# Routing shares brought to the rows of an expert tile by repeating DMA reads in place of a selection matmul

## The chip, the core and the metric

The kernel runs on one core of a Trainium2 chip, alone. The metric is the device time of one execution in microseconds (us). The engines named here are TensorE (PE, with PEld for its weight loads), VectorE (DVE), ScalarE (ACT), GpSimd (POOL) and SyncE (SP), whose queue issues the DMAs.

## What is computed

The program is a decoder of two layers over 32 sequences of 128 tokens with 128 features: attention, cross attention over a context and a feed forward part, twice, each added to x after a layer norm. The part that matters here is the last one, a mixture of experts on 4096 tokens:

```python
scores = sigmoid(x @ gate_w.T) + gate_bias                 # 64 experts
# the 4 best of 8 groups of experts, then the 6 best experts in them, their scores made to sum to 1
comb   = zeros((T, 64)).at[arange(T)[:, None], topk_i].add(topk_w)   # the routing shares
h      = silu(einsum('th,eih->eti', x, eg_w)) * einsum('th,eih->eti', x, eu_w)   # 64 hidden rows an expert
routed = einsum('eti,ehi,te->th', h, ed_w, comb)
shared = silu(x @ sg_w.T) * (x @ su_w.T) @ sd_w.T          # one expert of 128 rows for all tokens
x      = x + shared + routed
```

Every expert is computed for every token, and its hidden values are multiplied by the token's share for it, which is zero for 58 of 64 experts.

## The kernel before

Each engine has its own hand written order of work, and semaphores tie the orders together. The stages follow one another: attention, the wide cross attention, feed forward, attention, cross attention, experts. While the last cross attention runs, SP also loads the expert weights (`load_experts`, line 2096) and GpSimd splits each into a high part `w_hi`, rounded to fp32r, and the remainder `w_lo` (`split_experts`, line 639). A product in full precision is then three matmuls, high by high, high by low and low by high (`three`, line 1440).

The experts' stage takes the tokens in 8 groups (`G`) of 4 sequences, 512 tokens. Two experts of 64 rows make one tile of 128 partitions, so a group has 32 expert tiles and, as tile 32, the shared expert (`NT` = 33). For tile k the work is:

- TensorE, `project` (line 1445): three gate matmuls into one PSUM bank, three up matmuls into another, and for k < 32 one selection matmul (line 1461). Its weights `pick` are a 0/1 matrix that copies the high and the low part of the share of expert 2k to the upper 64 partitions and of expert 2k+1 to the lower 64, and sums them, into a third bank. Then `project_down` of tile k - 3 (`LAG` = 3): three matmuls.
- ACT: silu of the gate bank (line 1540), and `high_part` of tile k - 2, the copy of h to fp32r (`h_hi`, line 1547).
- VectorE: `product` of tile k, up bank times silu, into `h1` (line 1675); then `hidden` of tile k - 1 (line 1678), the share times `h1`, into `h` (line 1685); for tile 32 a plain copy (line 1688).
- GpSimd: `low_part`, h minus h_hi, into `h_lo` (line 1737), which the down matmuls need beside `h_hi`.

Everything in that list has two buffers by tile (`h_hi` and `h_lo` three): gate and up of tile k wait for silu and product of tile k - 2, the selection matmul for hidden of tile k - 2, hidden of tile k for h_lo of tile k - 2.

Beside this, group g prepares group g + 1: VectorE normalises it behind tile 2, TensorE transposes it behind tile 7 and computes the scores behind tile 9 (ACT changes its table to sigmoid and back there), GpSimd splits the inputs behind tile 10 (line 1731), VectorE does one of 16 routing steps behind each of the tiles 11 to 26 (`route`, line 1601). Behind tile 27 it splits the shares into a high and a low half (`split_shares`, lines 1665 and 1667), behind tile 29 TensorE transposes them (line 1436) and ACT copies them to `share_t` (line 1534). At the start of the stage all of that stands in line before tile 0 of group 0. SP only stores each finished group to the output (line 2117).

Of the kernel before, what the change touches and what calls it, by code (L numbers as in the profile page):

```python
# [638 lines left out]
def split_experts(pool, nc, m, s, k, u):  # L639

    at = slice(k * 128, k * 128 + 128) if isinstance(k, int) else bass.ds(k * 128, 128)
    pool.wait_ge(s.raw[u], 16 + 8 * (k - u))
    nc.gpsimd.tensor_copy(m.w_hi[:, :, at], m.raw[:, u, 0:3, :]).then_inc(s.split_hi, 1)
    if not (isinstance(k, int) and k == B):
        nc.gpsimd.tensor_copy(m.pick[:, at], m.raw[:, u, 3, :])
    pool.wait_ge(s.split_hi, k + 1)
    nc.gpsimd.tensor_tensor(m.w_lo[:, :, at], m.raw[:, u, 0:3, :], m.w_hi[:, :, at].bitcast(F32),
                            ALU.subtract).then_inc(s.split, 1)
# [388 lines left out]
GB = 4  # L1037
# [349 lines left out]
NT = E // 2 + 1  # L1387
LAG = 3
class ExpertSemaphores:

    def __init__(self, sem, stage):
        self.normed = sem(f"{stage}_normed")
        self.x_t = sem(f"{stage}_x_t")
        self.x_f = sem(f"{stage}_x_f")
        self.x_hi = sem(f"{stage}_x_hi")
        self.x_lo = sem(f"{stage}_x_lo")
        self.logits = sem(f"{stage}_logits")
        self.scores = sem(f"{stage}_scores")
        self.routed = sem(f"{stage}_routed")
        self.shares_t = sem(f"{stage}_shares_t")  # L1400
        self.shares = sem(f"{stage}_shares")
        self.gated = sem(f"{stage}_gated")
        self.upped = sem(f"{stage}_upped")
        self.shared_out = sem(f"{stage}_shared_out")
        self.silus = sem(f"{stage}_silus")
        self.products = sem(f"{stage}_products")
        self.hiddens = sem(f"{stage}_hiddens")
        self.his = sem(f"{stage}_his")
        self.los = sem(f"{stage}_los")
        self.downed = sem(f"{stage}_downed")  # L1410
        self.out_s = sem(f"{stage}_out_s")
        self.out_t = sem(f"{stage}_out_t")
        self.updated = sem(f"{stage}_updated")
# [4 lines left out]
def moe_tensor(pe, nc, m, s):  # L1418
# [14 lines left out]
    def transpose_shares(g):  # L1433
        pe.wait_ge(s.routed, g + 1)
        for q in range(GB):
            last = nc.tensor.transpose(m.misc[:, q * 128:q * 128 + 128], m.share[:, q, :].bitcast(F32),
                                       m.ident[:])
        last.then_inc(s.shares_t, 1)
# [6 lines left out]
    def project(g, u, k):  # L1445
        n, tile = NT * g + k, slice(128 * k, 128 * k + 128)
        if k == 0:
            pe.wait_ge(s.x_hi, g + 1)
            pe.wait_ge(s.x_lo, g + 1)
        wait(pe, s.silus, n - 1)  # L1450
        x_hi, x_lo = m.x_hi[:, u, :], m.x_lo[:, u, :]
        three(m.gate_bank[(k + u) % 2][:], m.w_hi[:, 0, tile], m.w_lo[:, 0, tile], x_hi, x_lo)\
            .then_inc(s.gated, 1)
        wait(pe, s.products, n - 1)
        three(m.up_bank[(k + u) % 2][:], m.w_hi[:, 1, tile], m.w_lo[:, 1, tile], x_hi, x_lo)\
            .then_inc(s.upped, 1)
        if k < NT - 1:
            wait(pe, s.hiddens, n - 1)
            if k == 0:
                pe.wait_ge(s.shares, g + 1)  # L1460
            nc.tensor.matmul(m.share_bank[(k + u) % 2][:], m.pick[:, tile], m.share_t[:, u, :],  # L1461
                             start=True, stop=True).then_inc(s.shared_out, 1)

# [15 lines left out]
    def body(g, u):  # L1479
        before, after = group_exists(g - 1), group_exists(g + 1)  # L1480
        for k in range(NT):
            project(g, u, k)
            if k >= LAG:
                project_down(g, k - LAG)
            elif before:
                project_down(g - 1, k - LAG + NT)
            if k == 5 and before:
                transpose_output(g - 1)
            if k == 7 and after:
                wait(pe, s.updated, GB * g)  # L1490
                transpose_inputs(g + 1)
            if k == 9 and after:
                logits(g + 1)
            if k == 29 and after:
                transpose_shares(g + 1)
# [25 lines left out]
def moe_scalar(act, nc, m, s):  # L1521
# [9 lines left out]

    def copy_shares(g, u):
        act.wait_ge(s.shares_t, g + 1)
        nc.scalar.copy(m.share_t[:, u, :], m.misc[:]).then_inc(s.shares, 1)

# [17 lines left out]
    def body(g, u):  # L1553
        before, after = group_exists(g - 1), group_exists(g + 1)
        for k in range(NT):
# [9 lines left out]
            if k == 9 and after:  # L1565
                routing_scores(g + 1)
            if k == 29 and after:
                copy_shares(g + 1, 1 - u)

    copy_inputs(0)  # L1570
    routing_scores(0)
    copy_shares(0, 0)
    over_groups(act, body)
# [8 lines left out]
def moe_vector(dve, nc, m, s):  # L1582
# [18 lines left out]
    def route(g, n):  # L1601
# [5 lines left out]
        if n == 0:  # L1607
            dve.wait_ge(s.scores, g + 1)
            last = nc.vector.tensor_tensor(rows(m.sc, E), rows(m.sg, E),
                                           m.gate_b[:].unsqueeze(1).broadcast_to([128, GB, E]), ALU.add)  # L1610
# [50 lines left out]

    def split_shares(g):
        dve.wait_ge(m.s.route, ROUTE_STEPS * (g + 1))
        wait(dve, s.shares_t, g)
        nc.vector.tensor_copy(m.share[:, :, 0:E], rows(m.w, E)).then_inc(m.s.halves, 1)
        dve.wait_ge(m.s.halves, g + 1)
        nc.vector.tensor_tensor(m.share[:, :, E:2 * E], rows(m.w, E), m.share[:, :, 0:E].bitcast(F32),
                                ALU.subtract).then_inc(s.routed, 1)

    def product(g, u, k):  # L1670
# [7 lines left out]
    def hidden(g, u, k):  # L1678
# [4 lines left out]
        if k < NT - 1:  # L1683
            dve.wait_ge(s.shared_out, (NT - 1) * g + k + 1)
            nc.vector.tensor_tensor(m.h[:, here, :], m.share_bank[here][:], m.h1[:, here, :], ALU.mult)\  # L1685
                .then_inc(s.hiddens, 1)
        else:
            nc.vector.tensor_copy(m.h[:, here, :], m.h1[:, here, :]).then_inc(s.hiddens, 1)
# [8 lines left out]
    def body(g, u):  # L1697
        before, after = group_exists(g - 1), group_exists(g + 1)
        for k in range(NT):
# [11 lines left out]
            if 11 <= k < 11 + ROUTE_STEPS and after:  # L1711
                route(g + 1, k - 11)
            if k == 27 and after:
                split_shares(g + 1)

    normalise(0)
    split_inputs(0, 0)
    for n in range(ROUTE_STEPS):
        route(0, n)
    split_shares(0)  # L1720
    over_groups(dve, body)
# [4 lines left out]
def moe_pool(pool, nc, m, s):  # L1726
# [24 lines left out]
    low_part(G - 1, 1, NT - 1)  # L1751

# [52 lines left out]
def program(nc, io, out):  # L1807
    arena = ExitStack()
    with arena:
# [88 lines left out]
        with ExitStack() as part:  # L1898
            over = placer(part)
            m.pick = over("pick", [128, (NT - 1) * 128], F32R)  # L1900
        m.score_w = sb("score_w", [128, XH, C])
        m.out_w = sb("out_w", [128, XH, C])

        with ExitStack() as part:
            over = placer(part)
            m.raw = over("raw", [128, 2, 4, 128])
        m.wug = sb("wug", [128, 2 * FT * C])
# [34 lines left out]
        with ExitStack() as part:  # L1942
# [4 lines left out]
            m.x_lo = over("x_lo", [128, 2, 512], F32R)  # L1947
            m.share_t = over("share_t", [128, 2, 512], F32R)
            m.share = over("share", [128, GB, 2 * E], F32R)
            m.sl = over("sl", [128, 2, 512])  # L1950
# [46 lines left out]
        m.mixed, m.back, m.asked = bank[4], bank[5], bank[7]  # L1997
        m.gate_bank, m.up_bank, m.share_bank, m.out_bank, m.misc = bank[0:2], bank[2:4], bank[4:6], bank[6], bank[7]

# [14 lines left out]
        m.s.route = sem("all_route")  # L2014
        m.s.halves = sem("all_halves")
        m.s.stored = sem("all_stored")
# [27 lines left out]
        for n, (a, a.k_diag, a.q_pack, a.v_store) in enumerate(stages):  # L2044
            a.q_rows, a.k_rows = (nc.dram_tensor(f"{side}_rows{n}", (2, HC, ROWS, NC, 2 * T), F32, kind="Internal").ap()
                                  for side in "qk")
            a.ones = nc.dram_tensor(f"ones{n}", (128 - MAXIMA, SLOTS * H * a.columns), F32, kind="Internal").ap()
            a.ones_in = 16 * (n + 1)

        def row(name, p=128):  # L2050
# [25 lines left out]
        with nc.Block() as block:  # L2076
            @block.sync
            def _(sp):
# [35 lines left out]
                load_experts(B, 0)  # L2114
                with sp.Fori(0, G) as g:
                    sp.wait_ge(s5.updated, GB * g + GB)
                    sp.dma_start(out[bass.ds(g * GB, GB)].rearrange("b t c -> t b c"),
                                 x_view[:, bass.ds(g * GB, GB), :]).then_inc(m.s.stored, 16)
                sp.wait_ge(m.s.stored, 16 * G)
# [136 lines left out]
def layouts(w):  # L2256
# [14 lines left out]
    def up(a, shared):  # L2271
        return np.concatenate([a.reshape(E // 2, 128, C), shared[None]]).transpose(0, 2, 1)

    down = np.concatenate([w["L1_ffn_ed_w"].reshape(E // 2, 2, C, 64).transpose(0, 1, 3, 2).reshape(E // 2, 128, C),
                           w["L1_ffn_sd_w"].T[None]])
    expert = 2 * np.arange(NT)[:, None] + np.arange(128)[None, :] // 64
    pick = (np.arange(128)[None, :, None] % E == expert[:, None, :]).astype(np.float32)
    experts = np.stack([up(w["L1_ffn_eg_w"], w["L1_ffn_sg_w"]), up(w["L1_ffn_eu_w"], w["L1_ffn_su_w"]),
                        down, pick], 2)
    out = {"bias_columns": np.concatenate([columns("L0_attn_b_attn", (0, 1)), columns("L1_xattn_bq", (0,)),  # L2280
# [29 lines left out]
```

## Time and profile before

| | |
|---|---|
| median of 3 runs | 2505.26 us (2498.2 to 2507.59) |
| profiled execution | 2503.74 us, span 2501.9 us |
| mean granted clock of TensorE | 0.923 |
| busy share of the span | PE 88%, PEld 73%, DVE 65%, ACT 56%, POOL 38% |
| selection matmul, line 1461 | 256 matmuls of 512 columns |
| experts' stage | from about 1853 us to the end |

The page gives busy time by engine, then the span in 40 slices, the DMA queues, the chain of work that ended last, and the costliest groups of instructions with what ended the idle time before them. "bank" is a PSUM bank. Matmuls are pipelined: the times at which they start tell more than their durations. An operation's duration includes the time in which it stands on its engine and can't read its operands.

### The profile page before, as it was taken

To read this page: it belongs to the slowest core of one execution; us is meant where nothing else is said; L and a number is where in the kernel's file an instruction comes from. 1 tells how busy PE (TensorE), PEld (TensorE's weight loads), DVE (VectorE), ACT (ScalarE), POOL (GpSimd) and SP (SyncE) were. 2 spreads that over 40 slices of the span, in tenths; PEclk is the share of its full clock that TensorE was granted. 3 is DMA by queue.
4 is the path that set the end of the run, shared out by engine and by line. 5 is a ranking of instruction groups with operands and counts; after the bars stand their busy time and mean duration, and the time that the engine had idled before them with its cause. 6 is when DMAs were issued, how large, how long until landed. Compare 5 with 4: busy or idle time off the path is not lost.

```text
span 2501.9 us, 52319 instructions
## 1 busy us (share of the span) xinstructions
PE 2194.1 (88%) x16155; PEld 1824.7 (73%) x16241; DVE 1634.5 (65%) x3705; ACT 1395.2 (56%) x3390; POOL 949.5 (38%) x1125
## 2 busy tenths in 40 slices
PE   1999989999999999970269999688879999999998
PEld 0677679999999999830147776466547888888887
DVE  2566657666776666679855665466547677776775
ACT  0455457777777777755415554355535555555554
POOL 2111124444444444305321110233315555555555
PEclk9999979999999999985569999588859999999999
DMA  8333300000000000000023332355510000000000
GB/s 201 121 121 120 100 1 2 0 0 0 0 0 0 0 0 0 1 0 0 0 77 104 116 120 71 105 152 153 149 32 1 5 5 6 2 4 5 5 5 5
DMA packets 178614, 111.78 MB, mean 45 GB/s; under 512 B 31619, under 2 KB 173891, under 8 KB 178371
## 3 DMA queue, kind: packets, MB, share of 16 engines
q1 hardware_dynamic: 178491, 110.30, 15.2%
q8 instruction: 57, 0.93, 0.2%
q14 instruction: 66, 0.54, 0.1%
HBM read 68.82 MB, written 42.10 MB: 44 GB/s over the span
## 4 chain that ended last, share of the span: by engine, by line
PE 79%; SPq 8%; DVE 6%; issue 3%; DMA 2%; ACT 1%; POOL 1%; DVEq 0%; POOLq 0%; ACTq 0%
PE bank L1441 7%; PE bank L1443 7%; PE bank L1442 7%; PE bank L239 6%; PE bank L719 5%; PE bank L720 5%; PE bank L721 5%; PE bank L713 5%; PE bank L764 4%; PE bank L742 4%; PE bank L250 4%; PE bank L221 3%; SPq L599 3%; PE bank L1461 2%; PE bank L237 2%
## 5 line engine op out<-in xcount | busy, mean ns | idle before, releaser
L1737 POOL TENSOR_TENSOR h_lo<-h,h_hi 128x512 fp32r<-128x512 f32 x264 | 340.5, 1290 | 284.8 <-ACT h_hi L1547 284.8
L427 DVE TENSOR_REDUCE nm<-bank 128x4 f32<-128x512 f32 (+1 forms) x384 | 238.0, 621 | 294.4 <-PE bank L221 293.2
L361 ACT ACTIVATE pt<-bank 128x512 f32<-128x512 f32 (+1 forms) x384 | 228.8, 596 | 285.9 <-PE bank L239 281.0
L982 POOL TENSOR_TENSOR pw<-ew,rw 128x410 f32<-128x410 f32 x256 | 223.2, 872 | 372.3 <-DVE rw L904 372.3
L1540 ACT ACTIVATE sl<-bank 128x512 f32<-128x512 f32 x264 | 157.9, 598 | 275.1 <-PE bank L1443 273.0
L1675 DVE TENSOR_TENSOR h<-bank,sl 128x512 f32<-128x512 f32 x264 | 182.0, 689 | 174.8 <-PE bank L1443 148.1
L239 PE MATMUL bank<-q_pack,k_diag 128*128 128x128 f32 (+1 forms) x1536 | 269.4, 302 | 24.3 <-DMA q_pack<-nmt 24.3
L239 PEld LDWEIGHTS bank<-q_pack,k_diag 128*128 128x128 f32 (+1 forms) x1536 | 215.6, 191 | 63.9 <-DMA q_pack<-nmt 25.8
L908 DVE TENSOR_TENSOR pwt_lo<-bank,pwt_hi 128x512 fp32r<-128x512 f32 x256 | 176.9, 691 | 78.9 <-ACT pwt_hi L836 78.8
L221 PE MATMUL bank<-k_diag,q_pack 128*128 128x512 f32 (+1 forms) x384 | 210.3, 552 | 13.9 <-DMA k_diag<-k_rows 12.0
L827 ACT ACTIVATE ew<-bank,nmax 128x205 f32<-128x205 f32 x512 | 217.7, 434 | 1.0 <-DVE nmax L896 0.9
L1441 PE MATMUL bank<-x_hi,w_hi 128*128 128x512 f32 x528 | 209.3, 396 | 0.0
L1443 PE MATMUL bank<-x_hi,w_lo 128*128 128x512 f32 x528 | 206.5, 391 | 0.0
L1442 PE MATMUL bank<-x_lo,w_hi 128*128 128x512 f32 x528 | 206.2, 391 | 0.0
L250 PE MATMUL bank<-pt,vx 128*32 128x128 f32 (+1 forms) x3072 | 172.7, 299 | 2.6 <-ACT pt L361 1.9
L1685 DVE TENSOR_TENSOR h<-bank,h 128x512 f32<-128x512 f32 x256 | 174.0, 680 | 0.2 <-DVE h L1675 0.2
L842 ACT COPY us<-bank 128x256 f32<-128x256 f32 x256 | 95.3, 372 | 124.7 <-PE bank L721 123.5
L1547 ACT CAST h_hi<-h 128x512 fp32r<-128x512 f32 x264 | 161.7, 612 | 3.2 <-DVE h L1685 1.6
L713 PE MATMUL bank<-kvt,score_w 128*128 128x128 f32 x1024 | 158.1, 277 | 1.7 <-DVE qs_lo L913 0.9
L719 PE MATMUL bank<-kvt_hi,qs_hi 128*128 128x206 f32 x512 | 158.8, 310 | 0.0
L546 POOL COPY vx<-v_store 128x128 f32 (+3 forms) x96 | 27.8, 290 | 344.5 <-PE bank L250 344.5
L742 PE MATMUL bank<-ident,pw 128*128 128x128 f32 x1024 | 154.2, 273 | 3.2 <-POOL pw L982 2.1
(278 smaller groups left out, 5962.3 us busy)
## 6 DMA issues: line engine op xcount, KB each, us to landing
q_pack<-q_rows SPq DMA_DIRECT2D x96, 256.0 KB, 3.1
k_diag<-k_rows SPq DMA_DIRECT2D x256, 64.0 KB, 2.6
q_rows<-q_hi SPq DMA_DIRECT2D x96, 128.0 KB, 2.1
k_rows<-k_hi SPq DMA_DIRECT2D x96, 128.0 KB, 2.1
raw<-in_experts SPq DMA_DIRECT2D x33, 256.0 KB, 2.7
q_rows<-q_lo SPq DMA_DIRECT2D x48, 128.0 KB, 2.1
k_rows<-k_lo SPq DMA_DIRECT2D x48, 128.0 KB, 2.1
k_diag<-k_rows SPq DMA_DIRECT2D x128, 39.0 KB, 2.5
```

The lines of the kernel that those rows point to most:

```text
L221: nc.tensor.matmul(bank, a.q_pack[:, u, c, :], a.k_diag[:, u, c, :, 0:a.columns], start=a.mask is None, stop=True)\
L239: last = nc.tensor.matmul(bank[0:a.keys, 128 * h:128 * h + 128], a.k_diag[:, u, c, h, 0:a.keys], a.q_pack[:, u, c, :], start=a.mask is Non ...
L250: last = nc.tensor.matmul(m.mixed[ROWS * h:ROWS * h + ROWS, 128 * c:128 * c + 128], m.vx[0:a.keys, u % 2, HC * c + h, :], m.pt[0:a.keys, c ...
L361: nc.scalar.activation(m.pt[0:a.keys, c % 2, :, :].rearrange("p h t -> p (h t)"), m.flip[c % 2][0:a.keys, :], ACT.Exp).then_inc(s.exped.se ...
L427: nc.vector.tensor_reduce(m.nm[:, u % 2, :].rearrange("p (h c) -> p c h", c=NC)[:, c, :], m.score[c % 2][:, 0:HC * a.columns].rearrange("p ...
L713: last = nc.tensor.matmul(m.ask[:, 128 * k:128 * k + 128], m.score_w[:, 2 * c + k, :], m.kvt[:, u, 0:T], start=True, stop=True)
L719: nc.tensor.matmul(out, left_hi, right_hi, start=first, stop=False)
L742: last = nc.tensor.transpose(m.flip[0][:, at:at + 128], m.pw[:, c % 2, k, 128 * part:128 * part + 128], m.ident[:])
L1441: nc.tensor.matmul(bank, w_hi, x_hi, start=first, stop=False)
L1442: nc.tensor.matmul(bank, w_hi, x_lo, start=False, stop=False)
L1443: return nc.tensor.matmul(bank, w_lo, x_hi, start=False, stop=last)
L1737: nc.gpsimd.tensor_tensor(m.h_lo[:, k % 3, :], m.h[:, (k + u) % 2, :], m.h_hi[:, k % 3, :].bitcast(F32), ALU.subtract).then_inc(s.los, 1)
```

## The change

The share no longer goes through TensorE. VectorE doesn't split the shares, and TensorE transposes the routing weights of two sequences at a time (2 transposes of 128 columns in place of 4), behind tile 28 in place of 29. ACT copies them to `share_t`, now 128x256 fp32. SP writes `share_t` to a DRAM scratch `share_rows` of 64 experts by 512 tokens with two DMAs, waits for both, and then, for each of the 32 tiles, issues one DMA that reads the two rows of the tile's experts 64 times over and writes 128 partitions of 512 fp32 values (256 KB) to one of four buffers, `share_b`. The load for tile k waits until hidden of tile k - 4 is done. VectorE's hidden of tile k waits for that load and multiplies `share_b` by `h1`; both of its inputs now lie in SBUF. The stores to the output move into the same row of SP's work, behind the load of tile 12 of the next group.

Because the repeated read gives expert 2k to the even partitions and expert 2k + 1 to the odd ones, the rows of the two experts of a tile are interleaved in the weights, on the host. The matrix `pick` is gone from the inputs: an expert's load has 192 KB in place of 256, and GpSimd's copy of it (line 645) goes.

```diff
-    nc.gpsimd.tensor_copy(m.w_hi[:, :, at], m.raw[:, u, 0:3, :]).then_inc(s.split_hi, 1)
-    if not (isinstance(k, int) and k == B):
-        nc.gpsimd.tensor_copy(m.pick[:, at], m.raw[:, u, 3, :])
+    nc.gpsimd.tensor_copy(m.w_hi[:, :, at], m.raw[:, u, :, :]).then_inc(s.split_hi, 1)
...
     def transpose_shares(g):
-        pe.wait_ge(s.routed, g + 1)
-        for q in range(GB):
-            last = nc.tensor.transpose(m.misc[:, q * 128:q * 128 + 128], m.share[:, q, :].bitcast(F32),
-                                       m.ident[:])
+        pe.wait_ge(m.s.route, ROUTE_STEPS * (g + 1))
+        for q in range(GB // 2):
+            last = nc.tensor.transpose(m.misc[:, q * 128:q * 128 + 128], m.w[:, q * 128:q * 128 + 128], m.ident[:])
         last.then_inc(s.shares_t, 1)
...
-        if k < NT - 1:
-            wait(pe, s.hiddens, n - 1)
-            if k == 0:
-                pe.wait_ge(s.shares, g + 1)
-            nc.tensor.matmul(m.share_bank[(k + u) % 2][:], m.pick[:, tile], m.share_t[:, u, :],
-                             start=True, stop=True).then_inc(s.shared_out, 1)
...
-            if k == 29 and after:
+            if k == 28 and after:
...
-    def copy_shares(g, u):
+    def copy_shares(g):
         act.wait_ge(s.shares_t, g + 1)
-        nc.scalar.copy(m.share_t[:, u, :], m.misc[:]).then_inc(s.shares, 1)
+        wait(act, s.rows_saved, 32 * g)
+        nc.scalar.copy(m.share_t[:], m.misc[:, 0:256]).then_inc(s.shares, 1)
...
-    def split_shares(g):
-        dve.wait_ge(m.s.route, ROUTE_STEPS * (g + 1))
-        wait(dve, s.shares_t, g)
-        nc.vector.tensor_copy(m.share[:, :, 0:E], rows(m.w, E)).then_inc(m.s.halves, 1)
-        dve.wait_ge(m.s.halves, g + 1)
-        nc.vector.tensor_tensor(m.share[:, :, E:2 * E], rows(m.w, E), m.share[:, :, 0:E].bitcast(F32),
-                                ALU.subtract).then_inc(s.routed, 1)
...
         if k < NT - 1:
-            dve.wait_ge(s.shared_out, (NT - 1) * g + k + 1)
-            nc.vector.tensor_tensor(m.h[:, here, :], m.share_bank[here][:], m.h1[:, here, :], ALU.mult)\
+            dve.wait_ge(s.share_in[k % SHARES], 16 * ((NT - 1) // SHARES * g + k // SHARES + 1))
+            nc.vector.tensor_tensor(m.h[:, here, :], m.share_b[:, k % SHARES, :], m.h1[:, here, :], ALU.mult)\
                 .then_inc(s.hiddens, 1)
...
+def moe_sync(sp, m, s, out, x_view):
+
+    def save_shares(g, u):
+        sp.wait_ge(s.shares, g + 1)
+        for k in range(2):
+            sp.dma_start(m.share_rows[u].rearrange("e (p k t) -> k e p t", k=2, t=T)[k],
+                         m.share_t[E * k:E * k + E, :]).then_inc(s.rows_saved, 16)
+
+    def load_share(g, u, k):
+        if k == 0:
+            sp.wait_ge(s.rows_saved, 32 * g + 32)
+        wait(sp, s.hiddens, NT * g + k - SHARES + (k >= SHARES))
+        pair = m.share_rows[u, 2 * k:2 * k + 2, :].rearrange("e t -> (e t)").unsqueeze(0).broadcast_to([64, 2 * 512])
+        sp.dma_start(m.share_b[:, k % SHARES, :], pair).then_inc(s.share_in[k % SHARES], 16)
+
+    def store(g):
+        sp.wait_ge(s.updated, GB * g + GB)
+        first = g * GB if isinstance(g, int) else None
+        dst = out[first:first + GB] if isinstance(g, int) else out[bass.ds(g * GB, GB)]
+        src = x_view[:, first:first + GB, :] if isinstance(g, int) else x_view[:, bass.ds(g * GB, GB), :]
+        sp.dma_start(dst.rearrange("b t c -> t b c"), src).then_inc(m.s.stored, 16)
+
+    def body(g, u):
+        save_shares(g, u)
+        for k in range(NT - 1):
+            load_share(g, u, k)
+            if k == 12 and group_exists(g - 1):
+                store(g - 1)
+
+    over_groups(sp, body)
+    store(G - 1)
...
-            m.pick = over("pick", [128, (NT - 1) * 128], F32R)
+            m.share_b = over("share_b", [128, SHARES, 512])
...
-            m.share_t = over("share_t", [128, 2, 512], F32R)
-            m.share = over("share", [128, GB, 2 * E], F32R)
+            m.share_t = over("share_t", [128, 256])
...
+        m.share_rows = nc.dram_tensor("share_rows", (2, E, 512), F32, kind="Internal").ap()
...
-        return np.concatenate([a.reshape(E // 2, 128, C), shared[None]]).transpose(0, 2, 1)
-
-    down = np.concatenate([w["L1_ffn_ed_w"].reshape(E // 2, 2, C, 64).transpose(0, 1, 3, 2).reshape(E // 2, 128, C),
+        pairs = a.reshape(E // 2, 2, 64, C).transpose(0, 2, 1, 3).reshape(E // 2, 128, C)
+        return np.concatenate([pairs, shared[None]]).transpose(0, 2, 1)
+
+    down = np.concatenate([w["L1_ffn_ed_w"].reshape(E // 2, 2, C, 64).transpose(0, 3, 1, 2).reshape(E // 2, 128, C),
                            w["L1_ffn_sd_w"].T[None]])
-    expert = 2 * np.arange(NT)[:, None] + np.arange(128)[None, :] // 64
-    pick = (np.arange(128)[None, :, None] % E == expert[:, None, :]).astype(np.float32)
     experts = np.stack([up(w["L1_ffn_eg_w"], w["L1_ffn_sg_w"]), up(w["L1_ffn_eu_w"], w["L1_ffn_su_w"]),
-                        down, pick], 2)
+                        down], 2)
```

## Rows read from the trace of the kernel before

**Rows 1.** Busy time by stretch: engines with counts, granted clock, DMA share, GB/s.

```profile
1872.30:2491.00 618.70, 617.21 (x2757) 504.87 (x2757) 446.69 (x826) 324.81 (x569) 346.40 (x268) 1.00 0.01 4
```

**Rows 2.** Order in time, TensorE, two group ends: start, us, engine, line, operation.

```profile
2040.55 0.60 PE L1475 MATMUL bank<-ident,yt 128*128 128x128 f32 x4
2040.90 0.48 PE L1441 MATMUL bank<-x_hi,w_hi 128*128 128x512 f32 x1
...
2118.38 0.60 PE L1475 MATMUL bank<-ident,yt 128*128 128x128 f32 x4
```

**Rows 3.** Order in time, all engines, one plain tile of group 2.

```profile
2100.15 0.39 PE L1441 MATMUL bank<-x_hi,w_hi 128*128 128x512 f32 x1
...
2101.03 0.60 ACT L1540 ACTIVATE sl<-bank 128x512 f32<-128x512 f32 x1 [1.17 <-PE bank L1443]
...
2101.52 0.61 ACT L1547 CAST h_hi<-h 128x512 fp32r<-128x512 f32 x1
2101.72 0.69 DVE L1675 TENSOR_TENSOR h<-bank,sl 128x512 f32<-128x512 f32 x1 [0.98 <-PE bank L1443]
...
2102.21 1.29 POOL L1737 TENSOR_TENSOR h_lo<-h,h_hi 128x512 fp32r<-128x512 f32 x1 [0.98 <-ACT h_hi L1547]
2102.32 0.68 DVE L1685 TENSOR_TENSOR h<-bank,h 128x512 f32<-128x512 f32 x1
...
2103.98 0.69 DVE L1675 TENSOR_TENSOR h<-bank,sl 128x512 f32<-128x512 f32 x1 [0.98 <-PE bank L1443]
```

**Rows 4.** The instructions of line 1643: ns least/median/most, first and last start.

```profile
L1643 DVE TENSOR_TENSOR sa<-ms,m x8: 426/862/862, 1864.3 to 2391.7; 128x256 f32<-128x256 f32 x8
```

**Rows 5.** Order in time, VectorE and GpSimd, a routing step of group 2.

```profile
2074.55 1.29 POOL L1737 TENSOR_TENSOR h_lo<-h,h_hi 128x512 fp32r<-128x512 f32 x1 [0.97 <-ACT h_hi L1547]
...
2075.26 0.86 DVE L1634 TENSOR_TENSOR ms<-sc,gq 128x256 f32<-128x256 f32 x1
```

**Rows 6.** Order in time, the last tile's plain copy.

```profile
2493.01 0.43 DVE L1688 COPY h<-h 128x512 f32<-128x512 f32 x1 [0.58 <-POOL h_lo L1737]
...
2493.16 2.65 POOL L1737 TENSOR_TENSOR h_lo<-h,h_hi 128x512 fp32r<-128x512 f32 x2 [0.26 <-ACT h_hi L1547]
...
2494.62 0.19 PEld L1441 LDWEIGHTS bank<-h_hi,w_hi 128*128 128x128 f32 x1 [1.13 <-POOL h_lo L1737]
```

**Rows 7.** Order in time, VectorE and GpSimd at a splitting of inputs.

```profile
2056.00 1.29 POOL L1737 TENSOR_TENSOR h_lo<-h,h_hi 128x512 fp32r<-128x512 f32 x1 [0.23 <-ACT h_hi L1547]
...
2056.61 0.97 DVE L1609 TENSOR_TENSOR sc<-sg,gate_b 128x256 f32<-128x256 f32 x1
...
2057.26 1.47 POOL L1731 TENSOR_TENSOR x_lo<-xf,x_hi 128x512 fp32r<-128x512 f32 x1
```

**Rows 8.** The tile raw: its instructions, ns least/median/most, and who waits.

```profile
L2099 SPq DMA_DIRECT2D raw<-in_experts x33: 328/430/765, 1607.1 to 1837.5; - x33
...
L645 POOL CAST pick<-raw x32: 288/291/295, 1610.5 to 1837.9; 128x128 f32 x20, 128x128 fp32r<-128x128 f32 x12
...
  DMA raw<-in_experts: 136.9, 29
```

**Rows 9.** DMA issues: count, KB each, median us to landing.

```profile
q_pack<-q_rows SPq DMA_DIRECT2D x96, 256.0 KB, 3.1
...
q_rows<-q_hi SPq DMA_DIRECT2D x96, 128.0 KB, 2.1
...
bases<-in_L_xattn_bproj SPq DMA_DIRECT2D x1, 64.0 KB, 3.0
```

**Rows 10.** Order in time, start of the experts' stage.

```profile
1868.86 0.43 DVE L1667 TENSOR_TENSOR share<-w,share 128x256 fp32r<-128x256 f32 x1
...
1869.35 1.12 PE L1436 MATMUL bank<-ident,share 128*128 128x128 f32 x4 [10.11 <-DVE share L1667]
...
1876.25 0.68 DVE L1685 TENSOR_TENSOR h<-bank,h 128x512 f32<-128x512 f32 x1
```

**Rows 11.** Busy time by stretch, in the cross attention.

```profile
1740.00:1760.00 20.00, 17.15 (x178) 12.30 (x181) 13.29 (x33) 11.23 (x25) 8.37 (x16) 0.89 0.49 142
```

More of the change, by code:

```diff
@@ L642, in split_experts @@
     pool.wait_ge(s.raw[u], 16 + 8 * (k - u))
-    nc.gpsimd.tensor_copy(m.w_hi[:, :, at], m.raw[:, u, 0:3, :]).then_inc(s.split_hi, 1)
-    if not (isinstance(k, int) and k == B):
-        nc.gpsimd.tensor_copy(m.pick[:, at], m.raw[:, u, 3, :])
+    nc.gpsimd.tensor_copy(m.w_hi[:, :, at], m.raw[:, u, :, :]).then_inc(s.split_hi, 1)
     pool.wait_ge(s.split_hi, k + 1)
-    nc.gpsimd.tensor_tensor(m.w_lo[:, :, at], m.raw[:, u, 0:3, :], m.w_hi[:, :, at].bitcast(F32),
+    nc.gpsimd.tensor_tensor(m.w_lo[:, :, at], m.raw[:, u, :, :], m.w_hi[:, :, at].bitcast(F32),
                             ALU.subtract).then_inc(s.split, 1)
@@ L1388 @@
 LAG = 3
+SHARES = 4
 class ExpertSemaphores:
@@ L1398, in __init__ @@
         self.scores = sem(f"{stage}_scores")
-        self.routed = sem(f"{stage}_routed")
         self.shares_t = sem(f"{stage}_shares_t")
@@ L1403, in __init__ @@
         self.upped = sem(f"{stage}_upped")
-        self.shared_out = sem(f"{stage}_shared_out")
+        self.rows_saved = sem(f"{stage}_rows_saved")
+        self.share_in = [sem(f"{stage}_share_in{k}") for k in range(SHARES)]
         self.silus = sem(f"{stage}_silus")
@@ L1566, in body @@
                 routing_scores(g + 1)
-            if k == 29 and after:
-                copy_shares(g + 1, 1 - u)
+            if k == 28 and after:
+                copy_shares(g + 1)
     copy_inputs(0)
     routing_scores(0)
-    copy_shares(0, 0)
+    copy_shares(0)
     over_groups(act, body)
@@ L1608, in route @@
             dve.wait_ge(s.scores, g + 1)
+            wait(dve, s.shares_t, g)
             last = nc.vector.tensor_tensor(rows(m.sc, E), rows(m.sg, E),
@@ L1712, in body @@
                 route(g + 1, k - 11)
-            if k == 27 and after:
-                split_shares(g + 1)
     normalise(0)
@@ L1719, in moe_vector @@
         route(0, n)
-    split_shares(0)
     over_groups(dve, body)
@@ L1905, in program @@
             over = placer(part)
-            m.raw = over("raw", [128, 2, 4, 128])
+            m.raw = over("raw", [128, 2, 3, 128])
         m.wug = sb("wug", [128, 2 * FT * C])
@@ L1997, in program @@
         m.mixed, m.back, m.asked = bank[4], bank[5], bank[7]
-        m.gate_bank, m.up_bank, m.share_bank, m.out_bank, m.misc = bank[0:2], bank[2:4], bank[4:6], bank[6], bank[7]
+        m.gate_bank, m.up_bank, m.out_bank, m.misc = bank[0:2], bank[2:4], bank[6], bank[7]
         m.s, m.es = Names(), Names()
@@ L2014, in program @@
         m.s.route = sem("all_route")
-        m.s.halves = sem("all_halves")
         m.s.stored = sem("all_stored")
@@ L2114, in _ @@
                 load_experts(B, 0)
[L2115 to L2118, printed above, removed]
+                moe_sync(sp, m, s5, out, x_view)
                 sp.wait_ge(m.s.stored, 16 * G)
```

## The prediction

> **What bounds the kernel now.** I read the 40 slices first, then the stage table, the groups by shape, and the order in time of single tiles. The change lies in the last stage, the experts (8 groups of 33 tiles), and in the copies made for it one stage earlier. From 1872 to 2491 us TensorE is busy 617.2 of 618.7 us at a granted clock of 1.00 (its 2.4 GHz level); VectorE is busy 72% and GpSimd 56% [rows 1]. A tile is a gapless row of ten 512-wide matmuls: three gate, three up, one selection, three down. VectorE's products of two tiles start 2.26 us apart (2101.72 to 2103.98), so a matmul is worth 0.226 us [rows 3]. The output transposes of two groups start at 2040.55 and 2118.38, so a group takes 77.8 us [rows 2].
>
> The reader must also see how little room there is beside TensorE. In [rows 3] the gate matmuls start at 2100.15, silu at 2101.03, the h_hi copy at 2101.52, the product at 2101.72, GpSimd's h_lo subtraction (1.29 us) at 2102.21, the multiplication by the share ("hidden") at 2102.32. The last two lie over each other, and hidden's 0.68 us doesn't suffer. Its inputs there are one PSUM bank and h1.
>
> **Part 1, the selection matmul goes.** 32 tiles x 8 groups = 256 matmuls x 0.2265 us = 58.0 us of TensorE, all on the path [rows 3]. Two of four share transposes a group go too: four took 0.35 us of the row (2040.55 to 2040.90) [rows 2], so 0.17 us x 8 = 1.4 us. With nothing else late, a tile takes 9 x 0.2265 = 2.04 us.
>
> **Part 2, hidden reads two SBUF tensors.** This decides the case. Before, the share came from PSUM; now share_b and h1 are both in SBUF, while h_lo (two SBUF inputs on GpSimd) runs beside it. The trace has this pair in another place, the routing. A 128x256 VectorE operation with two SBUF inputs takes 426 ns at least and 862 in the median of eight [rows 4]. The short ones lie at the start of the stage, where no h_lo runs yet (0.43 us at 1868.86 [rows 10]); in a running group the same kind starts at 2075.26 and ends at 2076.12, 0.28 us after the h_lo beside it (2074.55 + 1.29 = 2075.84) [rows 5]. Against 0.43 us for 256 elements, 0.69 us for 512 [rows 3] is 0.26 more, so I take hidden at 0.69 us when free and at 0.55 us after the end of h_lo when blocked.
>
> It works the other way round too. The copy of 2493.01 ends at 2493.44; the subtraction issued at 2493.16 frees its matmul only at 2494.62, so ends about 1.13 us after the copy [rows 6]. In [rows 7] the VectorE addition, issued at 2056.61 during an h_lo, ends at 2057.58, and the next GpSimd subtraction, issued at 2057.26, ends at 2058.73, 1.15 us later. Here VectorE got its turn between two GpSimd operations: who asks first goes first. So: blocked h_lo ends 1.15 us after VectorE's operation.
>
> The Trainium skill (SBUF — State Buffer, "Who interferes with whom") says the same of a VectorE operation with both inputs in SBUF against GpSimd's reads, and says the pair of ports is held for the whole instruction. The trace agrees on the blocking but not on the last point: taken literally, the blocked 256-wide operation would end 0.43 us after h_lo, and the row shows 0.28. By the page's version both blocked terms below would be 0.14 us longer, the cycle 7.41 us instead of 7.13, and the run some 24 us slower again.
>
> **The cycle that follows.** Waits in the code: down(k) needs h_lo(k), down(k) stands in TensorE's row behind up(k+3) and in front of gate(k+4), VectorE runs product(k+1), hidden(k), ACT runs silu(k+2), h_hi(k). Asked first, goes first: at a 2.04 us pace h_lo(k-2) asks 0.11 us before hidden(k-1), hidden is blocked, its h_hi and h_lo come late, and TensorE waits. Followed tile by tile it settles in a pattern of three tiles. From a late down(k), in us: three down matmuls 0.68; gate start to silu 0.89; silu to h_hi(k+2) 0.49; to h_lo(k+2) 0.69; h_lo 1.29; hidden(k+3), blocked by it, 0.55; handoff to the next product 0.05; to hidden(k+4) 0.60; which asks just before h_lo(k+3) and runs 0.69; blocked h_lo(k+3) 1.15; handoff to down(k+3) 0.05. Sum 7.13 us for three tiles: 2.38 a tile, against 2.26 before and 2.04 of matmuls, with TensorE waiting 1.0 us of every 7.1. Every term is from rows 3 to 7.
>
> I carried the same rules and durations tile by tile through whole groups, with routing steps, the plain copy of tile 32 and the two table loads of ACT in each group. For the kernel before they give 78.5 us a group (measured 77.8 [rows 2]), for the changed one 83.7: +5.2 us. The plain cycle alone gives 33 x 0.12 = 4 us of that; the rest is routing operations in the same queue for the port. Group 0 comes to +4.9, the last group (no routing) to +3.7: 4.9 + 6 x 5.2 + 3.7 = 39.8 us.
>
> Bounds: with the hold of either operation 0.1 us shorter the group comes to 81.0 (+2.5), with GpSimd favoured when both ask 88.1 (+9.6): +20 to +77 us in all. The outer bound below is no blocking at all, rival 1. I take the middle, since the rules meet the group of before within 0.7 us.
>
> **Part 3, the shares through DRAM.** SP has only eight stores in this stage. It now issues 32 loads and two saves a group, 272 in all, at the 0.43 us of an expert load's issue [rows 8]: 117 us in 620, on no other engine. A 256 KB load lands 3.1 us after issue, a save as large as 128 KB 2.1 [rows 9]; a 64 KB bias row repeated over the partitions took 3.0 [rows 9], so a repeated read shows no price of its own. Load k is issued when hidden(k-4) has ended and needed 4 x 2.38 - 0.69 = 8.8 us later. Cost 0; bounds 0 and rival 2. Behind a waiting load on SP stand later loads, the save for the next group and the store of out, which nothing waits for until the end. The last store stays behind the last update. At k = 0 of a later group the chain is transposes, copy, save 2.1, load 3.1, some 7 us, from tile 28 to hidden(0) behind product 1 of the next group, six tiles or 12 us: 0.
>
> At the start the split (its second operation 0.43) and half the slow transposes (1.12 for four) leave the path [rows 10]; save and load come on it. Transposes end near 1869.2, the copy near 1869.6, two saves issued and landed 1872.4, load 1875.5; hidden(0) ran at 1876.25 before [rows 10]. I take 0, bounds -1 and +3.
>
> **Part 4, smaller edits.** The split of the shares leaves VectorE (two operations like the 0.43 of [rows 10] a group): it lay beside matmuls, 0; uncovered it would be -7. The pick copy (0.29 us x 32) and 64 of 256 KB of each expert load leave the stage before. GpSimd waited there 136.9 us for the load, TensorE for other things than these copies [rows 8]: 0; bounds -3 and 0. The interleaved rows cost the same weights and matmuls: 0.
>
> **Sum.** 2503.7 (the profiled execution; span 2501.9) + 39.8 = 2543.5. The median of the three runs is 1.5 above that execution: 2545.
>
> **Rivals.**
> 1. *No blocking for hidden* (each keeps its own pace). Then TensorE is the bound: group 72.0 against 78.5 by the same arithmetic, -6.5 x 8 = -52: 2453. For it: no row shows a 512-wide hidden with two SBUF inputs. Against: rows 4 to 7. This is the other side; it turns where blocking adds less than 0.23 us a tile. Chance 0.14.
> 2. *The shares land late.* Decides above 8.8 us from hidden(k-4); at 12 us each tile takes 0.8 more, +205: 2750. Against it, the slowest row is 3.1. Chance 0.03.
> 3. *The clock falls.* TensorE gets gaps of 1.0 us. The stretch 1740 to 1760, busy 17.2 of 20, had a granted clock of 0.89 in the mean of the two levels 2.4 and 1.2 GHz [rows 11]. If it falls in a fifth of the stage, a tile there takes twice 2.04: 51 tiles x 1.7 = +87 on top: 2632. Against: here one gap of 1.0 us comes in every 7.1, and the stage of before held 1.00 through 1.5 us of gaps [rows 1]. Chance 0.05.
> 4. *The blocking is about worth the matmul*: hidden asks in the gap each time and only 0.22 us a tile is lost. Within 0.5% of before: 2505. Chance 0.06.
>
> The forecast has 0.72, and its own range 2515 to 2582 is from the +20 to +77 above, and a little under it. The whole range, 2497 to 2590, leaves out rivals 1 and 2 and half of 3. A change of 0.5% (12 us) is about what can be told from none. Faster 0.15, same 0.07, slower 0.78.
>
> **What will show it.** Right: hidden on VectorE at two durations, 0.69 and about 1.2 to 1.75; h_lo at 1.29 with some at 1.7; matmuls waiting for h_lo; TensorE idle or late by up to 1.0 us behind h_lo, some 10 to 14% of the stage; clock 1.00; groups 83 us apart; SP waits for hidden, never hidden for a load. Wrong: hidden at 0.69 throughout beside h_lo (then rival 1), or VectorE waiting for DMA (rival 2), or a granted clock under 1 (rival 3). The prediction as a whole is wrong if the group takes under 78 us.

## The result and the profile after

The changed kernel takes 2555.1 us (2552.1 to 2556.0) against 2501.7 us of the kernel before, run beside it: a ratio of 1.021 (95% interval 1.018 to 1.024), slower by 53 us. The prediction had 2545, which is 40 above the 2505 us that it started from. The profiled execution has a span of 2549.9 us.

The stage in question by stretch, columns as in [rows 1]:

```profile
1872.30:2538.00 665.70, 593.64 (x2467) 437.96 (x2466) 585.20 (x808) 332.34 (x562) 377.42 (x268) 1.00 0.33 104
```

TensorE's share fell from 99.8% to 89% and its granted clock stayed at 1.00. VectorE rose from 72% to 88% without more work: the time in which an operation stands blocked counts as busy. The output transposes of two groups, as in [rows 2], give the length of a group, 84.75 us against 77.83:

```profile
2047.23 0.60 PE L1469 MATMUL bank<-ident,yt 128*128 128x128 f32 x4
...
2131.98 0.60 PE L1469 MATMUL bank<-ident,yt 128*128 128x128 f32 x4
```

The tile share_b, with what waited for what (ns least/median/most, then idle us and times):

```profile
L1753 SPq DMA_DIRECT2D share_b<-share_rows x256: 512/513/727, 1864.9 to 2529.4; - x128
L1673 DVE TENSOR_TENSOR h<-share_b,h x256: 678/1584/1731, 1868.1 to 2537.4; 128x512 f32<-128x512 f32 x128
...
  DMA share_b<-share_rows: 1.3, 1
...
  ACT h_hi L1542: 77.0, 118
...
DMA to landing us min/median/max: 2.8/3.2/4.0
```

Here is the answer. The multiplication by the share took 0.68 us before [rows 3]; now it takes 0.68 at least, 1.58 in the median and 1.73 at most. The loads are not late: they land 3.2 us after issue, and VectorE waited for one of 256 loads, the first (1.3 us). The long waits of the stage (who waits for whom, us in total, times, longest):

```profile
ACT h_hi L1542 <- DVE h L1673: 75.5, 117, 1.4
...
PEld bank L1441 <- POOL h_lo L1722: 145.6, 191, 3.0
...
PE bank L1441 <- POOL h_lo L1722: 74.5, 126, 2.6
DVE h L1663 <- PE bank L1443: 53.0, 93, 1.1
```

TensorE and its weight loads stand for h_lo, the h_hi copies for the multiplication. Before, in the same view of the stage, these pairs were short:

```profile
PEld bank L1441 <- POOL h_lo L1737: 5.9, 11, 1.6
...
ACT h_hi L1547 <- DVE h L1685: 1.6, 2, 0.9
```

And last a stretch of plain tiles in group 7, in order of time:

```profile
2502.62 0.50 PE L1441 MATMUL bank<-h_hi,w_hi 128*128 128x512 f32 x1 [0.77 <-POOL h_lo L1722]
2502.66 1.71 DVE L1673 TENSOR_TENSOR h<-share_b,h 128x512 f32<-128x512 f32 x1
...
2502.96 0.39 PE L1442 MATMUL bank<-h_lo,w_hi 128*128 128x512 f32 x1
...
2503.43 0.39 PE L1441 MATMUL bank<-x_hi,w_hi 128*128 128x512 f32 x1
...
2504.32 0.60 ACT L1535 ACTIVATE sl<-bank 128x512 f32<-128x512 f32 x1 [2.00 <-PE bank L1443]
...
2504.81 0.61 ACT L1542 CAST h_hi<-h 128x512 fp32r<-128x512 f32 x1
...
2505.50 1.29 POOL L1722 TENSOR_TENSOR h_lo<-h,h_hi 128x512 fp32r<-128x512 f32 x1 [1.69 <-ACT h_hi L1542]
2505.61 1.73 DVE L1673 TENSOR_TENSOR h<-share_b,h 128x512 f32<-128x512 f32 x1
...
2507.47 0.69 DVE L1663 TENSOR_TENSOR h<-bank,sl 128x512 f32<-128x512 f32 x1
...
2508.07 3.07 POOL L1722 TENSOR_TENSOR h_lo<-h,h_hi 128x512 fp32r<-128x512 f32 x2 [1.28 <-ACT h_hi L1542]
2508.08 0.68 DVE L1673 TENSOR_TENSOR h<-share_b,h 128x512 f32<-128x512 f32 x1
...
2509.95 0.50 PE L1441 MATMUL bank<-h_hi,w_hi 128*128 128x512 f32 x1 [0.77 <-POOL h_lo L1722]
```

Every step of the predicted cycle can be read here. The subtraction of 2505.50 is first, so the multiplication of 2505.61 ends at 2507.34, 0.55 us behind the subtraction's end at 2506.79. Then the multiplication of 2508.08 is first: it takes its free 0.68 us, and the row shows two subtractions from 2508.07 in 3.07 us, where two free ones take some 2.55. (The two rows start 0.01 us apart, h_lo's earlier; that the multiplication went first is read from the durations.) The down matmuls start late at 2502.62 and again at 2509.95: 7.33 us for three tiles, where 7.13 were predicted.

### The profile page after: what moved, and what is told of

The parts are those of the page before. It is cut to its first block, busy times and chain, and to the rows that moved or that the text cites. A ratio compares the mean times of both kernels' runs of the same rounds, so it can differ in the third digit from the quotient of the medians.

```text
span 2549.9 us, 52079 instructions
## 1 busy us (share of the span) xinstructions
PE 2166.3 (85%) x15969; PEld 1756.2 (69%) x15969; DVE 1777.4 (70%) x3689; ACT 1406.7 (55%) x3390; POOL 978.0 (38%) x1093
## 4 chain that ended last, share of the span: by engine, by line
PE 56%; POOL 10%; issue 10%; DVE 9%; SPq 9%; DMA 3%; ACT 2%; POOLq 0%; DVEq 0%; ACTq 0%
POOL h_lo L1722 10%; PE bank L239 5%; PE bank L717 5%; PE bank L718 5%; PE bank L719 5%; PE bank L711 5%; PE bank L762 4%; PE bank L740 4%; PE bank L250 4%; SPq L599 3%; DVE h L1673 3%; PE bank L237 3%; PE bank L221 2%; SPq L575 2%; PE bank L220 2%
## 5 line engine op out<-in xcount | busy, mean ns | idle before, releaser
L1722 POOL TENSOR_TENSOR h_lo<-h,h_hi 128x512 fp32r<-128x512 f32 x264 | 374.1, 1424 | 305.7 <-ACT h_hi L1542 305.0
L1673 DVE TENSOR_TENSOR h<-share_b,h 128x512 f32<-128x512 f32 x256 | 345.4, 1349 | 4.8 <-DVE h L1663 1.3
L1441 PE MATMUL bank<-h_hi,w_hi 128*128 128x512 f32 x264 | 124.2, 470 | 74.6 <-POOL h_lo L1722 74.5
```

The source lines that it names most:

```text
L1441: nc.tensor.matmul(bank, w_hi, x_hi, start=first, stop=False)
L1673: nc.vector.tensor_tensor(m.h[:, here, :], m.share_b[:, k % SHARES, :], m.h1[:, here, :], ALU.mult)\
L1722: nc.gpsimd.tensor_tensor(m.h_lo[:, k % 3, :], m.h[:, (k + u) % 2, :], m.h_hi[:, k % 3, :].bitcast(F32), ALU.subtract).then_inc(s.los, 1)
```

## Experiments

The theory throughout: hidden with two SBUF inputs and the h_lo subtraction on GpSimd shut each other out, first come, first served, and TensorE pays behind h_lo. The rivals: the repeated loads are late or their traffic slows an engine; the interleaving or SP's new work costs it; hidden is slow with two SBUF inputs whatever GpSimd does. The kernel before ran beside each set, at 2500.8 us (e1 to e4) and 2499.9 us (e5 to e7). All kernels but e3 start from the changed one. e2 and e6 multiply by whatever lies in share_b, e3 leaves the shares out, and e4 half of the low parts: their results are not those of the program, and only their times count.

**e1, h1 in PSUM.** One of hidden's two inputs moves to the two banks that the selection matmul left free.

```diff
-        nc.vector.tensor_tensor(m.h1[:, (k + u) % 2, :], m.up_bank[(k + u) % 2][:],
+        nc.vector.tensor_tensor(m.h1_bank[(k + u) % 2][:], m.up_bank[(k + u) % 2][:],
                                 m.sl[:, (k + u) % 2, :], ALU.mult).then_inc(s.products, 1)
...
-            nc.vector.tensor_tensor(m.h[:, here, :], m.share_b[:, k % SHARES, :], m.h1[:, here, :], ALU.mult)\
+            nc.vector.tensor_tensor(m.h[:, here, :], m.share_b[:, k % SHARES, :], m.h1_bank[here][:], ALU.mult)\
...
+        m.h1_bank = bank[4:6]
```

> The changed kernel with one edit: VectorE writes h1, the product of up and silu, to a PSUM bank instead of SBUF, so that hidden reads one SBUF tensor (share_b) and one bank. All DMAs, waits and matmuls stay. Theory (hidden with two SBUF inputs and the h_lo subtraction on GpSimd shut each other out): hidden at 0.68 us throughout, h_lo at 1.29, a group 71.8 us instead of 84.8, some 2448 us in all, so below both kernels. Rival (the repeated loads are late, or their 256 KB a tile slow the engines): no change, 2555, groups 85. Rival (the interleaved weights or the waits of SP cost it): 2555.

Measured: 2460.0 us, ratio to the kernel before 0.984 (0.982 to 0.987). That is 95 us off the changed kernel and 41 us under the kernel before. The pair in order of time, from one tile to the next:

```profile
2099.36 1.30 POOL L1722 TENSOR_TENSOR h_lo<-h,h_hi 128x512 fp32r<-128x512 f32 x1 [1.33 <-ACT h_hi L1542]
...
2099.47 0.68 DVE L1673 TENSOR_TENSOR h<-share_b,bank 128x512 f32<-128x512 f32 x1
...
2101.42 1.29 POOL L1722 TENSOR_TENSOR h_lo<-h,h_hi 128x512 fp32r<-128x512 f32 x1 [0.76 <-ACT h_hi L1542]
...
2101.53 0.68 DVE L1673 TENSOR_TENSOR h<-share_b,bank 128x512 f32<-128x512 f32 x1
```

The subtraction and the multiplication lie over each other as in [rows 3], at 1.29 and 0.68 us, 2.06 us a tile. The stage by stretch, and the output transposes, 72.81 us apart:

```profile
1872.30:2440.00 567.70, 559.51 (x2442) 431.84 (x2443) 425.22 (x803) 316.75 (x557) 342.69 (x265) 1.00 0.40 122
```

```profile
2024.03 0.60 PE L1469 MATMUL bank<-ident,yt 128*128 128x128 f32 x4
...
2096.84 0.60 PE L1469 MATMUL bank<-ident,yt 128*128 128x128 f32 x4
```

Same DMAs, same interleaving, same work of SP: those rivals fall. It is 12 us more than the 2448 expected, with a group at 72.8 for 71.8. The wait that is left:

```profile
PEld bank L1441 <- POOL h_lo L1722: 53.0, 185, 1.7
```

The weights of the down matmuls wait 0.29 us in most tiles, as h_lo now comes only just in time at 2.06 us a tile.

**e2, no loads.** The first four share loads of group 0 are made and the other 252 left out.

```diff
-            load_share(g, u, k)
+            if isinstance(g, int) and g == 0 and k < SHARES:
+                load_share(g, u, k)
...
-            dve.wait_ge(s.share_in[k % SHARES], 16 * ((NT - 1) // SHARES * g + k // SHARES + 1))
+            dve.wait_ge(s.share_in[k % SHARES], 16)
```

> The changed kernel with only the first four share loads of group 0; all 252 others are left out and hidden reads what lies in share_b, so the shares are not those of the routing. Both inputs of hidden stay in SBUF. Theory (VectorE and GpSimd shut each other out): no gain, 2555 within 5 us, hidden's durations spread from 0.68 to 1.7 us as before. Rival (late loads or the DMA traffic): 2450.

Measured: 2556.2 us, ratio 1.022 (1.019 to 1.025). Without the traffic nothing is won, and the multiplication is as slow as with it:

```profile
L1673 DVE TENSOR_TENSOR h<-share_b,h x256: 676/1647/1766, 1873.2 to 2542.4; 128x512 f32<-128x512 f32 x128
```

**e3, the pair in the kernel before.** Nothing of the change but one operand: another SBUF tensor stands where the bank of the share stood.

```diff
-            nc.vector.tensor_tensor(m.h[:, here, :], m.share_bank[here][:], m.h1[:, here, :], ALU.mult)\
+            nc.vector.tensor_tensor(m.h[:, here, :], m.x_hi[:, u, :].bitcast(F32), m.h1[:, here, :], ALU.mult)\
```

> The kernel before, selection matmul and its waits kept, but hidden multiplies h1 by x_hi, an SBUF tensor, instead of by the bank of the share (the shares are left out of the result). No DMA is added. Theory: the blocking alone, with ten matmuls a tile: group 77.8 + 8.6 = 86.4 us by the rules of the prediction, 2502 + 69 = 2571 us. Rival (DMA): as before, 2502.

Measured: 2570.6 us, ratio 1.029 (1.027 to 1.032): 70 us for the blocking with no DMA added, where 69 were expected. The multiplication, and the first line of who waited for it:

```profile
L1685 DVE TENSOR_TENSOR h<-x_hi,h x256: 680/1562/1736, 1872.2 to 2555.9; 128x512 f32<-128x512 f32 x128
...
  PEld bank L1461: 81.4, 149
```

That line also shows where e3 differs from the changed kernel. L1461 is the selection matmul, which waits for the multiplication two tiles back; here most of TensorE's waiting stands there (81.4 us) and only 22.9 us of its weight loads' waits are for h_lo, where the changed kernel, which has no selection matmul, waits for h_lo. So e3 shows that the pair by itself makes the kernel slow, and not what each path costs in the changed kernel. Between the two kernels lie some 15 us, of the 58 that the selection matmul was worth.

**e4, half of h_lo.** GpSimd subtracts 256 of the 512 columns in all tiles but the first three.

```diff
-        nc.gpsimd.tensor_tensor(m.h_lo[:, k % 3, :], m.h[:, (k + u) % 2, :],
-                                m.h_hi[:, k % 3, :].bitcast(F32), ALU.subtract).then_inc(s.los, 1)
+        at = slice(0, 512 if isinstance(g, int) and g == 0 and k < 3 else 256)
+        nc.gpsimd.tensor_tensor(m.h_lo[:, k % 3, at], m.h[:, (k + u) % 2, at],
+                                m.h_hi[:, k % 3, at].bitcast(F32), ALU.subtract).then_inc(s.los, 1)
```

> The changed kernel, but GpSimd's h_lo subtraction covers only 256 of 512 columns (in all tiles but the first three), so it holds the ports about half as long; half of the low parts are left out of the result. In the kernel before its 1.29 us ended ahead of the down matmuls, so by itself it was not on the path. Theory: group 71.7 us, 2450 in all, because a blocked hidden then waits at most 0.6 us and TensorE's 2.04 us a tile bound again. Rival (DMA): 2555. Rival (hidden itself is slower with two SBUF inputs, whatever GpSimd does): 2555.

Measured: 2450.2 us, ratio 0.980 (0.977 to 0.982), as expected. Hidden is still blocked, but for less:

```profile
L1673 DVE TENSOR_TENSOR h<-share_b,h x256: 670/1171/1224, 1870.0 to 2439.3; 128x512 f32<-128x512 f32 x128
```

A multiplication of 1.17 us leaves the kernel 51 us under the one before, one of 1.58 us puts it 53 over. So a slow multiplication is not the price in itself; TensorE pays when h_lo comes late. (A subtraction of 256 columns is itself shorter, 0.74 us in the median for 1.29, and e4 doesn't part this from the shorter blocking.) The rival that hidden is slow by its own inputs falls too: its length follows GpSimd's.

**e5, two buffers.** On top of e1, `SHARES = 2` in place of 4.

```diff
-SHARES = 4
+SHARES = 2
```

> h1 in PSUM and two share buffers in place of four: the load of tile k can be issued only when hidden of tile k - 2 has ended. That leaves 2 x 2.2 - 0.7 = 3.7 us for a wait of SP, an issue of 0.5 us and a landing of 3.2 us after issue. Theory (the loads are hidden by four buffers, with some 4 us to spare): here the spare is used up, 0 to 0.25 us a tile more than with four, 2460 to 2520 us, and VectorE shows waits for the DMA of share_b. Rival (the loads cost something by their traffic, not by their distance): 2460, no waits for DMA.

Measured: 2464.1 us, ratio 0.985 (0.983 to 0.987), at the low end of what was expected and not told apart from e1's 2460.0. The groups are 72.8 us as in e1. At half the distance the loads are all but hidden:

```profile
L1673 DVE TENSOR_TENSOR h<-share_b,bank x256: 666/677/690, 1877.6 to 2454.1; 128x512 f32<-128x512 f32 x128
...
  DMA share_b<-share_rows: 5.9, 14
...
DMA to landing us min/median/max: 2.8/3.2/3.9
```

14 waits, 5.9 us in all. I had counted the spare as used up; it was just enough.

**e6, h1 in PSUM and no loads.** e1 with the edits of e2.

```diff
+            if isinstance(g, int) and g == 0 and k < SHARES:
+                load_share(g, u, k)
```

> h1 in PSUM, and only the first four share loads are made (the shares are not those of the routing). With the blocking gone TensorE paces the stage, so a price of the loads, if there is one, would show here. Theory (loads cost nothing): 2460, groups 72.8 us. Rival (256 KB a tile slow some engine or the weight loads of TensorE that now wait 0.28 us a tile): 2450 or less, groups 71.8.

Measured: 2459.7 us, ratio 0.983 (0.982 to 0.985), e1's time within what can be told. Two output transposes, 72.91 us apart:

```profile
2025.78 0.60 PE L1469 MATMUL bank<-ident,yt 128*128 128x128 f32 x4
...
2098.69 0.60 PE L1469 MATMUL bank<-ident,yt 128*128 128x128 f32 x4
```

So 66 MB of repeated reads (252 x 256 KB) beside a nearly full TensorE cost nothing that can be measured, with or without the blocking, and they are not behind the last us of e1's groups.

**e7, h_hi ahead of silu.** On top of e1, to bring h_lo forward.

```diff
-            silu(g, u, k)
             if k > 1:
                 high_part(g, u, k - 2)
             elif before:
                 high_part(g - 1, 1 - u, NT - 2 + k)
+            silu(g, u, k)
```

> h1 in PSUM, and ACT does h_hi of tile k - 2 ahead of silu of tile k instead of behind it. With h1 in PSUM the weight load of the down matmuls still waits for h_lo in 186 of 264 tiles, 0.28 us each; here h_lo comes about 0.5 us earlier and silu 0.5 us later. Theory (what is left above 9 matmuls a tile is h_lo coming late, and each such wait costs a restart of some 0.1 us): groups 71.8 to 72.3 us, 2450 to 2456, the waits for h_lo gone. Rival (silu now comes late for product and gate): 2460 or slower.

Measured: 2555.7 us, ratio 1.023 (1.021 to 1.024): 96 us slower than e1, a plain miss. In order of time:

```profile
2180.15 0.68 DVE L1673 TENSOR_TENSOR h<-share_b,bank 128x512 f32<-128x512 f32 x1
...
2180.86 0.62 ACT L1542 CAST h_hi<-h 128x512 fp32r<-128x512 f32 x1 [1.41 <-DVE h L1673]
...
2181.39 0.59 ACT L1535 ACTIVATE sl<-bank 128x512 f32<-128x512 f32 x1
...
2182.07 0.70 DVE L1663 TENSOR_TENSOR bank<-bank,sl 128x512 f32<-128x512 f32 x1 [0.84 <-ACT sl L1535]
...
2182.68 0.68 DVE L1673 TENSOR_TENSOR h<-share_b,bank 128x512 f32<-128x512 f32 x1
...
2183.39 0.62 ACT L1542 CAST h_hi<-h 128x512 fp32r<-128x512 f32 x1 [1.41 <-DVE h L1673]
```

h_hi of tile k - 2 waits for hidden(k - 2), silu(k) stands behind it on ACT, product(k) waits for silu(k), and hidden(k - 1) stands behind product(k) on VectorE, for which the next h_hi waits. The order closed a ring that advances one tile a turn: from the end of the multiplication 0.03 to h_hi, 0.53 to silu, 0.68 to the product, 0.61 to the next multiplication, and its 0.68 make 2.53 us, the step from 2180.86 to 2183.39. 33 such steps are 83.5 us of a group's 85.1. With silu in front, silu(k) stands behind h_hi(k - 3) instead of h_hi(k - 2): by the waits in the code the ring is still there, but one turn advances two tiles, some 1.3 us a tile, and TensorE's 2.06 bind. I had weighed that silu comes 0.5 us later, and not what it then waits for.

## Why the prediction was right

**Part 2, the blocking,** held: both ways, first come first served, ends 0.55 us behind the subtraction or (with the handoff) 1.19 behind the multiplication, 2508.76 to 2509.95. Over the whole trace of the changed kernel the two overlap in 254 tiles. In 187 the subtraction starts 0.11 us or more ahead, and the multiplication always ends 0.54 or 0.55 behind it; in the other 67 the multiplication goes first. In 56 of these the subtraction's row starts 0.01 us earlier, so who asked first can't be read from the rows to 0.01 us. e1, e3 and e4 show the blocking by itself, from both sides. The Trainium skill (SBUF — State Buffer, "Who interferes with whom") is right on who blocks whom. On its hold for the whole instruction the measurement decides again: by the literal reading a 512-wide multiplication would end 0.69 us behind the subtraction, and it ends 0.55 behind.

**The cycle** is there, three tiles long, with the same order of who goes first, but not everywhere. Of the 261 steps from one down matmul to the third after it, 88 lie within 0.01 us of 7.33, 20 of them in the last group and 8 to 11 in each of the others. The cycle is 2.44 us a tile, and a group of 84.75 us has 2.57. Term by term from the stretch shown: down to gate 0.81 (predicted 0.68), gate to h_hi 1.38 (1.38), to h_lo 0.69 (0.69), h_lo 1.29 (1.29), blocked hidden 0.55 (0.55), handoff 0.13 (0.05), product to hidden 0.61 (0.60), hidden 0.68 and blocked h_lo with handoff 1.19 (1.89 for both). Sum 7.33 against 7.13. By group the growth was 6.9 us where 5.2 were predicted (the forecast of 83.7 us looks nearer to 84.75 because the same rules had the group of before 0.7 too long), and in the last group, which has no routing, 6.7 (67.3 to 74.0) where 3.7 were predicted.

**The mis-sized term** is the restart of the down matmuls, and beside it the handoff. I took three down matmuls at 3 x 0.226 us also behind a wait. From a first matmul whose weights had to wait to the second it is 0.34 us (2502.62 to 2502.96) instead of 0.23, and the three take 0.81. That is 0.13 us in three tiles; the handoff adds 0.08, and the other terms take 0.01 off. 0.20 in three tiles is 0.067 a tile and, if it is carried to all 256 tiles, 17 us: 39.8 + 17 = 57 us. The stage, from its first normalisation to the end of the span, grew from 647.7 us (1854.2 to 2501.9) to 703.2 (1846.7 to 2549.9), by 55.5. The split into these two terms is read from one stretch, carried to tiles that don't run this cycle, and not tested by a kernel of its own. The step of 0.34 us was there to be read before: it stands behind 11 of the down matmuls of the kernel before.

**Part 1.** The 58 us of matmuls and the transposes did leave TensorE. Without the blocking they pay: a group of e1 is 5.0 us shorter than before, 40 us in eight, of the 52 in rival 1. e1 still has a wait for h_lo in most tiles, and rival 1 left its restarts out. Added up over e1's trace, the steps from first to second down matmul are 12.5 us longer than 0.2265 each (1.0 us before), and the first ones start 10.2 us late in all. That is enough for the missing 12 us; no kernel without these waits was run, so it is argued, not shown.

**Part 3.** Costs nothing that can be measured, as said: hidden(0) ran 21.4 us after the first normalisation (before 22.0), landing 3.2 us; an issue took SP 0.51 us for the 0.43 assumed, on no other engine. **Part 4.** The stage before can't tell: the experts' stage began between 1846.3 and 1856.1 us in the nine profiles, with no order by kernel.

**Rivals.** 1, no blocking: fell (e2, e3), and e1 is what it would have looked like. 2, late loads: fell (one wait; e2, e5, e6). 3, a lower clock: did not come, 1.00 from 1872 to 2538 us. 4, blocking worth the matmul: fell; in e3 it costs 70 us, and the matmul was worth 58.

## What to carry to other kernels

When a VectorE operand moves from PSUM to SBUF, count the SBUF inputs of that operation and look at what GpSimd does in the same microsecond: with two, the engines take turns, and the routing steps of this very kernel showed it beforehand, as one operation with two durations. The cure is cheap if a bank is free: write an intermediate that only VectorE reads back to PSUM, and the change that cost 53 us gains 41.

The count of inputs doesn't cover plain copies. The copy of tile 32 has one fp32 input, and it was blocked too: before, it took 0.43 us at least and 1.36 in the median, ending 0.28 us behind the subtraction. With its input in a bank (e1) it took 0.68 each time:

```profile
L1688 DVE COPY h<-h x8: 426/1361/1457, 1951.1 to 2493.0; 128x512 f32<-128x512 f32 x8
```

```profile
L1676 DVE COPY h<-bank x8: 680/681/693, 1940.7 to 2447.9; 128x512 f32<-128x512 f32 x8
```

And draw the waits as a ring before reordering two operations of one engine: a swap that moves nothing by more than half a microsecond can shorten a ring from two tiles a turn to one, and then the ring sets the pace.

## What was not expected of the hardware

- TensorE pays for a wait beyond the wait: 0.34 us to the second matmul behind held-up weights against 0.23 in the row, some 0.1 us each time (0.31 to 0.34), 190 times in the changed kernel. In e1, where the weights are less late, the step lies anywhere from 0.23 to 0.34.
- A load of 256 KB that reads 4 KB of DRAM 64 times over lands in 3.2 us, nearly as fast as one that reads 256 KB once (3.1, [rows 9]), and two buffers all but hide it at 2.2 us a tile (e5). Its issue takes SP 0.51 us, against 0.43 for an expert load.
- VectorE's product written to PSUM took 0.70 us against 0.69 to SBUF.
